# Stacked parts of q and k and rows of routing weights fetched by DMA instead of made by matmuls

## The chip, the cores and the metric

One core of a Trainium2 chip runs the whole kernel. The metric is the device time of one execution in microseconds. The engines run their own instruction streams in order and meet at semaphores: TensorE (PE in the profile), VectorE (DVE), ScalarE (ACT), GpSimd (POOL), and SyncE (SP), which issues DMAs.

## The reference

The input x is 4 batches of 1024 rows of 128 values. Each row is normalised (xn), and two branches work on it; the result is x + s * g.

```python
xn = _layernorm(x, axis=-1)
s = _L0_attn_ref(xn, ...)            # 16 heads of 8 values; q, k, v = xn @ w_qkv + b_qkv
g = _silu(_L0_ffn_ref(xn, ...))      # 16 experts of 64 hidden values, 4 chosen for a row, and a shared one of 128
# attention: heads 0 to 3 causal over all rows; heads 4 to 15 causal over the last 33 rows
# experts: scores = sigmoid(xn @ gate_w.T); the best 2 of 4 groups, in them the best 4 experts,
#          cw = their normalised scores * 2.5, 0 for the rest
y = jnp.einsum('nei,ne,ehi->nh', silu(hg) * hu, cw, Wd)
```

## The kernel before, in words

A batch is handled as two chunks of 512 rows (`CH`); features lie on the 128 partitions, rows on the free axis. The 16 heads are four groups `g` of four; groups 0 to 2 have the windowed heads, group 3 (`GLOBAL`) the causal ones. Each engine walks the same list of steps (`at.steps`) and carries out its own part of each. The list is written out by hand as strings of letters (`FIRST_ORDER`, `BODY_ORDER`, `LAST_ORDER`, L147 to L154), which weave streams: P prepares the next batch, A makes the operands of a group, R is scores and weighted values, X the experts, T the routing, V the values, C the division by the sums, 0 and 1 the output of a chunk. The start is one such list (67 us long), then the middle list runs for batches 0 to 2, each with the preparation of the next batch and its first six expert pairs in it, then the last list.

**Parts of q and k.** Products of q and k must be nearly exact in float16. So q is held as a high part `qkh` and a rest `qkl`, each 128 features by 1024 rows. For a group of four heads an operand has 32 rows for a head: 8 rows for each of three parts (q: high, rest, high; k: high, high, rest), and 8 rows of which one is the constant 1 in k and takes the negative row maximum in q. Before the change TensorE builds these with 0/1 matrices: `qsel` and `ksel` (L614, L615) are two matmuls a chunk, `x_a` with `qkh` and `x_b` with `qkl`, into a PSUM bank that ScalarE copies to `qtmp` and `kall` (L877, L879; for k it adds the constant row). Then `pads` has VectorE spread `qtmp` to the block form `qpad` (L1048), `max` multiplies it with `kall` and takes row maxima (L1144, L1146), `maxdone` has GpSimd lay the maxima on a diagonal (L1211), and `qfull` (L609, L610) adds them to q for the operand `qall`, which `score` uses (L659, L671); `kpads` is VectorE's copy of `kall` to blocks (L1061).

**Experts.** For a pair of experts `up` makes gate and up products, three matmuls each (L513 to L515). ScalarE applies tanh (L809), VectorE forms the product (L1100, then L1109, shown as L916 since a helper records it), GpSimd multiplies it with the routing weights (L1220), and `down` multiplies with `down_w` (L746). The weights `cw` of 16 experts are transposed to `cwT` (`cwT`, L595), with a rest computed by VectorE (L1139), and for a pair one matmul (L730) with `pairsel` spreads two rows of `cwT` over 64 partitions each; ScalarE copies it to `wrow` (L815). Thus an expert step takes three tiles of a ring of three PSUM banks (`EXP`), and the tiles of attention take turns on three others (`ATT`).

**DMAs.** SP loads the inputs, and per batch the next `xin` (L485), `xres` (L488), and two stores of the output (L491).

Of the kernel before, what the change touches and what calls it, by code (L numbers as in the profile page):

```python
# [16 lines left out]
F32 = mybir.dt.float32  # L17
F32R = mybir.dt.float32r
# [39 lines left out]
NWT = 3  # L58
SPLIT_PAIR = 6
XSLOTS = 3  # L60
ROUTE_PARTS = 7
# [3 lines left out]
C16 = {"q_a": HG * P, "q_b": HG * P, "k_a": HG * P, "k_b": HG * P, "negmax": P, "eye": P}  # L65
# [69 lines left out]
def expert_steps(c):  # L135
    out = []
    for t in range(NUP + LAG_DOWN):
# [4 lines left out]
        if t >= LAG_DOWN:  # L142
# [4 lines left out]
FIRST_ORDER = ("PIPPIIIPPPIITPPITPIPTITIPPTPIPPTIPPPPPTIPPIITTVXXVXVXXVXVXVXXXVVXXVXVXX")  # L147
BODY_ORDER = ("AAPAARXAAXAXRRARRAAARAAAAXXRPAAARAAXAXAARRAXRRAAAARRRAXAARAAPXARAAAAAAAXAAARXAAARAXAAAAXXRRRARAR"
              "RAAARAAAAARRARRAAARRRARAXARAAXAXRRRRARAPRAARXRRRRAAAARRRXAXRAXRRRAXRRARARAARPRRPARAXRRXXRTRXRRRR"
              "RTPRTRRRRPRRTXRRRRRRXXXRXRCRPRPRRRXXXRPPRPRRRRRPRRRTPCRRXXRPRRRRRTRRXPRXPRXRPPRRRRRXRRRTXXRRRRRT"  # L150
              "TRPCXPC00XVXXVXXVVVX01XXXX1X1VXVVVVXX")
LAST_ORDER = ("AAAAAAAXAARAARAAAXXRARXRAAAAARRARAAAXAXRRRAXARXAXARAARAAARRARAAAAAAAAAXAARAXAAAXXARAXRRRARRARAAA"
              "RAAAARARAAXRARRXRRRXRRRAAAAAAAARAAAARAAARAXRAXRRAXAAXRRRRAARRXRRRXRRRRRRRRAAXRRRXRXCXRRRRXCRRRRR"
              "RRRRRRXXRRRRRRRXRRRRXRRXRRRRXXRRRRXRRRRR0RXXRRRRRRRXRRRRRRXRRRRRRRXXR0XCC0111")  # L154
# [57 lines left out]
class Section:  # L212
# [5 lines left out]
    def __init__(self, steps):  # L218
# [3 lines left out]
        for s in steps:  # L222
# [8 lines left out]
            if s[0] in ("pv", "down", "norm", "qpads", "z", "z2", "ln", "stats", "pads", "kpads", "maxdone", "ctx", "route", "times",  # L231
                        "mul", "setup", "fill", "ones"):
                continue
            ahead = s[0] in ("qsel", "ksel", "max") and s[1] == 0
            ring = EXP if s[0] in ("up", "weights", "xT", "q", "k", "gate") or ahead else ATT
            parts = [s] if s[0] != "up" else [s + (x,) for x in ("weight", "gate", "up") if x != "weight" or s[2] < EP]
# [48 lines left out]
def build(nc, x, w_qkv, b_qkv, w_out, b_out, gate_w, gate_bias, Wg, Wu, Wd, Ws_g, Ws_u, Ws_d,  # L285
          c32, c16, out):
    with ExitStack() as ctx:
# [16 lines left out]
        def const16(name, g=0):  # L304
            return k16[:, f16at[name][0] + g * P:f16at[name][0] + (g + 1) * P]
# [24 lines left out]
        pairsel = sb("pairsel", [P, EP, P], F32R)  # L330
# [16 lines left out]
        qkl = sb("qkl", [P, 2, S], F16)  # L347
# [954 lines left out]
```

## Time and profile before

| | us |
|---|---|
| median of 3 runs (579.01 to 580.9) | 579.53 |
| the profiled execution | 581.03 |
| its span, first to last instruction | 579.2 |
| TensorE busy | 516.5 |
| VectorE busy | 429.8 |
| ScalarE busy | 332.7 |
| GpSimd busy | 179.6 |

The profile is of one execution. A busy time is the time in which an engine had at least one instruction at work; matmuls overlap, so their durations do not add up to it. The clock that is given for TensorE is the share of full speed that was granted.

### The profile page before, as it was taken

To read this page: it belongs to the slowest core of one execution; us is meant where nothing else is said; L and a number is where in the kernel's file an instruction comes from. 1 tells how busy PE (TensorE), PEld (TensorE's weight loads), DVE (VectorE), ACT (ScalarE), POOL (GpSimd) and SP (SyncE) were. 2 spreads that over 40 slices of the span, in tenths; PEclk is the share of its full clock that TensorE was granted. 3 is DMA by queue.
4 is the path that set the end of the run, shared out by engine and by line. 5 is a ranking of instruction groups with operands and counts; after the bars stand their busy time and mean duration, and the time that the engine had idled before them with its cause. 6 is when DMAs were issued, how large, how long until landed. Compare 5 with 4: busy or idle time off the path is not lost.

```text
span 579.2 us, 10586 instructions
## 1 busy us (share of the span) xinstructions
PE 516.5 (89%) x3930; PEld 301.7 (52%) x3960; DVE 429.8 (74%) x937; ACT 332.7 (57%) x646; POOL 179.6 (31%) x167
## 2 busy tenths in 40 slices
PE   1768999899998999899998999999998999989992
PEld 1636665555445665555445655545454755644440
DVE  6786697786698788886789788786779776877423
ACT  3544556656855457555865367564875457455851
POOL 3413431033524441024423442023342632003311
PEclk9957999998999999998999999998999999999996
DMA  9200000000000300000000300000000110000001
GB/s 233 73 1 0 2 1 1 2 1 2 0 1 2 110 2 2 1 1 1 1 2 1 94 16 3 1 1 1 1 2 0 37 38 1 3 1 0 1 1 36
DMA packets 17933, 9.82 MB, mean 17 GB/s; under 512 B 2502, under 2 KB 17754, under 8 KB 17882
## 3 DMA queue, kind: packets, MB, share of 16 engines
q1 hardware_dynamic: 17552, 8.85, 5.6%
q8 instruction: 31, 0.51, 0.4%
q10 hardware_dynamic: 330, 0.30, 0.3%
q14 instruction: 20, 0.16, 0.1%
HBM read 7.05 MB, written 2.10 MB: 16 GB/s over the span
## 4 chain that ended last, share of the span: by engine, by line
PE 48%; DVE 32%; issue 7%; ACT 6%; DVEq 3%; POOL 2%; DMA 1%; POOLq 0%; ACTq 0%
PE bank L746 6%; DVE kpad L1061 4%; DVE mxp L1146 4%; PE bank L629 4%; DVE mxp L1144 4%; PE bank L513 4%; PE bank L515 4%; PE bank L514 4%; PE bank L690 3%; DVE qpad L1048 3%; PE bank L659 3%; PE bank L706 3%; DVE denT L1085 3%; PE bank L730 2%; DVE hid L1100 2%
## 5 line engine op out<-in xcount | busy, mean ns | idle before, releaser
L889 ACT ACTIVATE stage<-bank 128x512 f32<-128x512 f32 (+3 forms) x240 | 112.7, 521 | 62.8 <-PE bank L663 41.7
L1220 POOL TENSOR_TENSOR hid<-hid,wrow 128x512 f32<-128x512 f32 x64 | 82.2, 1286 | 171.6 <-DVE hid L916 171.6
L1144 DVE TENSOR_REDUCE mxp<-bank 128x1 f32<-128x512 f32 (+4 forms) x192 | 89.8, 517 | 14.0 <-PE bank L632 8.2
L1100 DVE SCALAR_TENSOR_TENSOR hid<-hid,bank 128x512 f32<-128x512 f32 x72 | 48.9, 680 | 54.7 <-ACT hid L809 54.5
L746 PE MATMUL bank<-hid,down_w 128*128 128x512 f32 x144 | 76.0, 609 | 0.0
L1211 POOL TENSOR_TENSOR maxd<-mxp,k 128x512 f16<-128x512 f32 x32 | 36.4, 1137 | 117.9 <-DVE mxp L1146 64.0
L809 ACT ACTIVATE hid<-bank 128x512 f32<-128x512 f32 x72 | 43.3, 601 | 48.2 <-PE bank L515 47.4
L513 PE MATMUL bank<-xh,up_hi 128*128 128x512 f32 x144 | 60.8, 422 | 2.4 <-DVE hid L916 1.8
L514 PE MATMUL bank<-xh,up_lo 128*128 128x512 f32 x144 | 57.8, 401 | 0.0
L515 PE MATMUL bank<-xl,up_hi 128*128 128x512 f32 x144 | 57.4, 399 | 0.0
L659 PE MATMUL bank<-kpad,kall 128*128 128x512 f16 (+3 forms) x192 | 54.8, 329 | 2.1 <-ACT stage L889 1.7
L629 PE MATMUL bank<-kall,qpad 128*128 128x512 f16 (+4 forms) x192 | 50.5, 317 | 5.7 <-DVE mxp L1144 2.6
L916 DVE TENSOR_TENSOR hid<-hid,bank 128x512 f32<-128x512 f32 x72 | 48.9, 679 | 1.3
L659 PEld LDWEIGHTS bank<-kpad,kall 128*128 128x128 f16 x192 | 17.8, 97 | 44.9 <-issue 25.4
L690 PE MATMUL bank<-stage,vg 128*32 128x512 f32 (+3 forms) x384 | 40.0, 497 | 0.0
L815 ACT ACTIVATE wrow<-bank 128x512 f32<-128x512 f32 x64 | 38.1, 596 | 2.8 <-PE bank L730 2.8
L1048 DVE COPY qpad<-qtmp 32x1024 f16<-32x1024 f16 x64 | 29.7, 464 | 12.0 <-ACT qtmp L877 11.3
L730 PE MATMUL bank<-cwT,pairsel 128*128 128x512 f32 x64 | 33.7, 526 | 3.6 <-DVE hid L916 3.1
L882 ACT ACTIVATE qall<-bank 128x512 f16<-128x512 f32 x32 | 18.7, 597 | 31.2 <-PE bank L610 31.2
L513 PEld LDWEIGHTS bank<-xh,up_hi 128*128 128x128 f32 x144 | 28.2, 196 | 11.8 <-DVE hid L916 5.0
L1146 DVE TENSOR_REDUCE mxp<-bank 128x8 f32<-128x512 f32 x48 | 31.9, 686 | 2.8 <-PE bank L641 2.0
L629 PEld LDWEIGHTS bank<-kall,qpad 128*128 128x128 f16 x192 | 17.0, 96 | 31.9 <-DVE mxp L1144 17.4
(162 smaller groups left out, 1002.4 us busy)
## 6 DMA issues: line engine op xcount, KB each, us to landing
xin<-in_L_attn_x_dram SPq DMA_DIRECT2D x4, 512.0 KB, 4.2
xres<-in_L_attn_x_dram SPq DMA_DIRECT2D x4, 512.0 KB, 4.1
out_dram<-xres SPq DMA_DIRECT2D x8, 256.0 KB, 2.3
k<-in_c_dram SPq DMA_DIRECT2D x1, 576.0 KB, 5.8
stage<-in_L_ffn_Wg_dram SPq DMA_DIRECT2D x1, 512.0 KB, 6.0
stage<-in_L_ffn_Wu_dram SPq DMA_DIRECT2D x1, 512.0 KB, 5.9
stage<-in_L_ffn_Wd_dram SPq DMA_DIRECT2D x1, 512.0 KB, 7.4
k<-in_c_dram ACTq DMA_DIRECT2D x1, 216.5 KB, 3.9
```

Of the source, the lines that this page charges most:

```text
L513: pe.matmul(ps[:], w_hi, x_hi, start=True, stop=False)
L514: pe.matmul(ps[:], w_lo, x_hi, start=False, stop=False)
L515: return pe.matmul(ps[:], w_hi, x_lo, start=False, stop=True)
L629: ins = pe.matmul(ps[:, 0:cols], qpad[:, j, :, :], kall[:, g % 2, CH * c:CH * c + cols], start=True, stop=not last, skip_group_check=True)
L659: ins = pe.matmul(ps[:, 0:cols], kall[:, g % 2, P * j:P * (j + 1)], kpad[:, g % 2, q0 // BLK:(q0 + cols) // BLK, h, :], start=True, stop=n ...
L690: ins = pe.matmul(acc[BLK * h:BLK * (h + 1), q0 - CH * c:q0 - CH * c + cols], vg[:, j, h, :], prob[:, (SCORES_BEFORE[g] + m) % NPROB, 0:cols],
L746: pe.matmul(banks[Y][:], down_w[:, t, :], hid[:, i % NHID, :], start=(t == 0), stop=(t == NUP - 1)).then_inc(down_done, 1)
L889: act.activation(prob[:, t % NPROB, 0:cols], ps[:, 0:cols], ACT.Exp).then_inc(freed, 1)
L1100: dve.scalar_tensor_tensor(out=hid[:, i % NHID, :], in0=hid[:, i % NHID, :], scalar=1.0, in1=banks[at.bank(gate)][:], op0=ALU.add, op1=ALU ...
L1144: ins = dve.tensor_reduce(mxp[:, c, j:j + 1], ps[:, 0:cols], AX_X, ALU.max)
L1146: ins = dve.tensor_reduce(mxp[:, 0, LOC * n:LOC * (n + 1)], ps[:].rearrange("p (j q) -> p j q", q=2 * BLK), AX_X, ALU.max)
L1220: pool.tensor_tensor(hid[:, i % NHID, :], hid[:, i % NHID, :], wrow[:, iw % NWT, :], ALU.mult)\
```

## The change

The high parts and rests of q and k of a batch are stored to a DRAM tensor `planes` (for each head four parts of 8 rows), and both operands of a group come back as one transfer each (`strips`), already stacked, since in `planes` the rows of a head stand one behind the other. The fourth part, zeros for q and the constant row for k, is stored once at the start. `qtmp` gets two slots. The routing weights (`cwT`, 16 rows, in float32, halved by ScalarE) are stored to `cw_rows`, and a pair's rows are loaded to `wrow` with each row repeated over 64 partitions; one load covers two pairs, and three such slots are in use. The matmuls L614, L615 and L730, ScalarE's copies of their results (L815, L877, L879) and VectorE's subtraction for `cwT` (L1139) go, as do `pairsel` and the selection matrices. An expert step takes two tiles of its ring. All three orders are written anew. ScalarE and GpSimd get waits before they write what SP still may read. SP now walks the steps too.

```diff
-NWT = 3
+NWS = 3
+LOADS = NCH * EP // 2
+PARTS = 4
...
-C16 = {"q_a": HG * P, "q_b": HG * P, "k_a": HG * P, "k_b": HG * P, "negmax": P, "eye": P}
+C16 = {"negmax": P, "eye": P}
...
-    return ([("qsel", g, c) for c in range(NCH)] + [("ksel", g, c) for c in range(NCH)] + [("pads", g)]
-            + maxes[:half] + [("maxdone", g, 0)] + made + maxes[half:] + [("maxdone", g, 1)])
+    return ([("strips", g), ("pads", g)] + maxes[:half] + [("maxdone", g, 0)] + made + maxes[half:] + [("maxdone", g, 1)])
...
+        def written(b):
+            return 16 * (4 + 6 * b)
...
+            sp.wait_ge(plane_ready, 1)
+            for u in range(2):
+                for w, plane in enumerate((kpad[:, 1].rearrange("p j h q -> p (j h q)")[:, 0:S], maxd[:].rearrange("p j q -> p (j q)"))):
+                    sp.dma_start(planes[2 * u + w, :, PARTS - 1, :, :], plane).then_inc(planes_written, 16)
+
+            def load_weights(n):
+
+                c, t, slot = n // (EP // 2), 2 * (n % (EP // 2)), n % NWS
+                for side in range(2):
+                    row = cw_rows[2 * t + side:2 * t + side + 3:2, chunk(c)]
+                    sp.dma_start(wrow[64 * side:64 * side + 64, 2 * slot:2 * slot + 2, :],
+                                 row.unsqueeze(0).broadcast_to([64, 2, CH])).then_inc(wrow_loaded[slot], 16)
...
+                if at.section is not FIRST:
+                    for c in range(NCH):
+                        sp.wait_ge(stored[c], 16 * b + 16)
+                    sp.dma_start(xres[:], of_batch(x_v, b)).then_inc(xres_loaded, 16)
+                for s in at.steps:
+                    kind = s[0]
+                    if kind in ("q", "k") and s[1] == 1:
+                        w, to = "qk".index(kind), 2 * (at.next % 2) + "qk".index(kind)
+                        sp.wait_ge(lo_ready, at.next * 2 * NCH + (NCH + w + 1))
+                        for part, own in enumerate((qkh, qkl, qkh) if w == 0 else (qkh, qkh, qkl)):
+                            sp.dma_start(planes[to, :, part, :, :], own[:, w, :]).then_inc(planes_written, 16)
+                    elif kind == "strips":
+                        g = s[1]
+                        of, heads = b if g else at.next, slice(4 * HEADS[g], 4 * (HEADS[g] + 1))
+                        sp.wait_ge(planes_written, written(of + 1))
+                        if at.section is not FIRST:
+                            used = ("qfull", (g + 2) % HG, 1) if g != 1 else ("qfull", 0, 0)
+                            sp.wait_ge(emptied[at.bank(used)], at.taken(used))
+                            if g != 1:
+                                sp.wait_ge(kpad_ready, b * GLOBAL + (g - 1 if g else GLOBAL))
+                        for w, to in enumerate((qtmp, kall)):
+                            sp.dma_start(to[:, g % 2, :], planes[2 * (of % 2) + w, heads]
+                                         .rearrange("h a d q -> (h a d) q")).then_inc(strips_loaded[g % 2], 16)
+                    elif kind == "cwT":
+                        c = s[1]
+                        sp.wait_ge(emptied[at.bank(s)], at.taken(s))
+                        sp.dma_start(cw_rows[:, chunk(c)], cwT[:, chunk(c)]).then_inc(cw_rows_stored, 16)
+                        if c == NCH - 1:
+                            sp.wait_ge(cw_rows_stored, 16 * NCH * (at.next + 1))
+                            if at.next:
+                                sp.wait_ge(hid_ready, at.next * NCH * EP)
+                            for n in range(NWS):
+                                load_weights(n)
+                    elif kind == "times" and s[2] < EP and s[2] % 2:
+                        n = (EP * s[1] + s[2]) // 2 + NWS
+                        if n < LOADS:
+                            sp.wait_ge(hid_ready, at.of(s) * NCH * EP + (EP * s[1] + s[2] + 1))
+                            load_weights(n)
...
-                        else:
-                            n = "qk"[w]
-                            pe.matmul(ps[:], const16(n + "_a", g), qkh[:, w, chunk(c)], start=True, stop=False)
-                            ins = pe.matmul(ps[:], const16(n + "_b", g), qkl[:, w, chunk(c)], start=False, stop=True)
...
-                            if x == "weight" and t < EP:
-                                if first:
-                                    all_taken(pe, at, [("cwT", i) for i in range(NCH)])
-                                ps = fill(at, s + (x,))
-                                done(at, s + (x,), pe.matmul(ps[:], pairsel[:, t, :], cwT[:, chunk(c)], start=True, stop=True))
...
-                            act.activation(wrow[:, iw % NWT, :], banks[at.bank(weight)][:], ACT.Copy)\
-                                .then_inc(emptied[at.bank(weight)], 1)
...
+                        elif at.next:
+                            act.wait_ge(planes_written, written(at.next))
...
+                        act.wait_ge(lo_ready, 2 * NCH * (b + (2 if at.section is BODY else 1)))
                         act.activation(sT[:, chunk(s[1])], ps[:], ACT.Identity, bias=bs[:], scale=0.5).then_inc(freed, 1)
...
-                        all_taken(dve, at, [("qsel", g, i) for i in range(NCH)])
+                        dve.wait_ge(strips_loaded[g % 2], 2 * 16 * ((b if g else at.next) * HG // 2 + g // 2 + 1))
...
-                            tt(cwT[32:32 + E, chunk(c)], ps[0:E, :], cwT[0:E, chunk(c)].bitcast(F32), ALU.subtract).then_inc(freed, 1)
...
+                        slot = n % NWS
+                        pool.wait_ge(wrow_loaded[slot], 32 * (at.of(s) * LOADS_OF[slot] + n // NWS + 1))
```

Where the steps stand in the new middle list (the position of 313; before there were 325): `qfull` 0 of the batch 0 and 4, `up` pair 6 at 1, the statistics of the next x at 2, `strips` 1 at 6, `pads` 1 at 9, `up` pair 7 at 10, the first `max` of group 1 at 13, `strips` 2 and `pads` 2 at 30 and 32, `strips` 3 and `pads` 3 at 52 and 53; `q` and `k` of the next batch's second chunk at 194 and 198, `strips` 0 at 202 and `pads` 0 at 234; `cwT` at 274 and 275, `up` pairs 0 to 5 between 281 and 303, the last `times` at 305, and seven steps of V behind it.

## Rows read from the trace of the kernel before

**Rows 1.** The page's part 1: busy time, share of the span, instructions
```profile
PE 516.5 (89%) x3930; PEld 301.7 (52%) x3960; DVE 429.8 (74%) x937; ACT 332.7 (57%) x646; POOL 179.6 (31%) x167
```

**Rows 2.** Windows by batch: stretch, its us, busy us of each engine, clock, DMA
```profile
199.60:332.30 132.70, 124.47 (x975) 72.90 (x982) 104.95 (x231) 80.41 (x157) 43.77 (x37) 0.99 0.05 13
465.00:579.20 114.20, 98.14 (x810) 50.93 (x814) 66.73 (x120) 62.42 (x124) 26.03 (x23) 0.95 0.03 9
0.00:66.90 66.90, 44.63 (x199) 32.20 (x201) 47.80 (x127) 29.14 (x51) 22.17 (x33) 0.85 0.26 67
```

**Rows 3.** Windows, two parts of one middle batch
```profile
200.00:264.00 64.00, 59.52 (x623) 35.59 (x627) 53.47 (x124) 39.02 (x74) 16.46 (x13) 1.00 0.02 6
264.00:332.00 68.00, 64.26 (x353) 37.09 (x352) 50.78 (x107) 41.39 (x83) 27.31 (x24) 0.97 0.06 16
```

**Rows 4.** The page's part 4, chain that ended last, by engine
```profile
PE 48%; DVE 32%; issue 7%; ACT 6%; DVEq 3%; POOL 2%; DMA 1%; POOLq 0%; ACTq 0%
```

**Rows 5.** Groups of TensorE by form: busy us, mean ns | idle before
```profile
L614 PE MATMUL bank<-qkh,k 128*128 128x512 f16 x64 | 25.3, 396 | 2.5 <-DVE up_lo L916 2.2 <-issue 0.2
L615 PE MATMUL bank<-qkl,k 128*128 128x512 f16 x64 | 25.3, 395 | 0.0
L730 PE MATMUL bank<-cwT,pairsel 128*128 128x512 f32 x64 | 33.7, 526 | 3.6 <-DVE hid L916 3.1 <-ACT wrow L815 0.3
```

**Rows 6.** The chain in order of time: start us, us, what
```profile
200.65 0.22 PE bank L614
200.87 0.22 PE bank L615
...
202.10 0.31 PE bank L730
202.41 0.23 PE bank L513
```

**Rows 7.** Groups of ScalarE by form
```profile
L815 ACT ACTIVATE wrow<-bank 128x512 f32<-128x512 f32 x64 | 38.1, 596 | 2.8 <-PE bank L730 2.8
L879 ACT ACTIVATE kall<-bank,k 128x512 f16<-128x512 f32 x32 | 21.1, 692 | 6.9 <-PE bank L615 6.5
L877 ACT ACTIVATE qtmp<-bank 128x512 f16<-128x512 f32 x32 | 17.5, 601 | 4.7 <-PE bank L615 4.7
```

**Rows 8.** Groups of VectorE by form
```profile
L916 DVE TENSOR_TENSOR cwT<-bank,cwT 16x512 fp32r<-16x512 f32 x8 | 5.2, 676 | 2.2 <-ACT cwT L856 2.2
L1048 DVE COPY qpad<-qtmp 32x1024 f16<-32x1024 f16 x64 | 29.7, 464 | 12.0 <-ACT qtmp L877 11.3
```

**Rows 9.** The page's part 6: DMA issues, KB each, us to landing
```profile
xin<-in_L_attn_x_dram SPq DMA_DIRECT2D x4, 512.0 KB, 4.2
out_dram<-xres SPq DMA_DIRECT2D x8, 256.0 KB, 2.3
```

**Rows 10.** Timelines of one batch turn: start us, us, engine, line
```profile
176.45 1.05 ACT L856 ACTIVATE cwT<-bank 16x512 fp32r<-16x512 f32 x2
...
185.00 2.56 POOL L1220 TENSOR_TENSOR hid<-hid,wrow 128x512 f32<-128x512 f32 x2
...
195.65 0.51 SPq L485 DMA_DIRECT2D xin<-in_L_attn_x_dram  x1
...
199.63 0.38 PE L609 MATMUL bank<-qtmp,k 128*128 128x512 f16 x1
...
204.37 1.71 DVE L1048 COPY qpad<-qtmp 32x1024 f16<-32x1024 f16 x4
```

**Rows 11.** Windows: the start's DMA, and where the granted clock fell
```profile
6.00:12.00 6.00, 0.68 (x3) 0.60 (x3) 5.18 (x25) 1.65 (x4) 1.65 (x1) 1.00 1.14 313
27.00:30.00 3.00, 1.13 (x7) 0.60 (x6) 2.61 (x8) 2.03 (x4) 1.45 (x2) 0.92 0.00 0
30.00:33.00 3.00, 1.82 (x4) 0.13 (x2) 2.61 (x15) 0.99 (x2) 0.00 (x0) 0.50 0.00 0
268.00:270.00 2.00, 2.00 (x4) 0.69 (x4) 1.14 (x4) 1.02 (x2) 0.63 (x1) 0.62 0.00 0
```

More of the change, by code:

```diff
@@ L231, in __init__ @@
             if s[0] in ("pv", "down", "norm", "qpads", "z", "z2", "ln", "stats", "pads", "kpads", "maxdone", "ctx", "route", "times",
-                        "mul", "setup", "fill", "ones"):
+                        "mul", "strips", "setup", "fill", "ones"):
                 continue
-            ahead = s[0] in ("qsel", "ksel", "max") and s[1] == 0
+            ahead = s[0] == "max" and s[1] == 0
             ring = EXP if s[0] in ("up", "weights", "xT", "q", "k", "gate") or ahead else ATT
-            parts = [s] if s[0] != "up" else [s + (x,) for x in ("weight", "gate", "up") if x != "weight" or s[2] < EP]
+            parts = [s] if s[0] != "up" else [s + (x,) for x in ("gate", "up")]
             for part in parts:
@@ L402, in build @@
         sums_ready = sem("sums_ready")
-        cw_hi_ready = sem("cw_hi_ready")
+        cw_rows_stored = sem("cw_rows_stored")
+        wrow_loaded = [sem(f"wrow{slot}_loaded") for slot in range(NWS)]
         small_loaded = sem("small_loaded")
@@ L419, in build @@
         kpad_ready = sem("kpad_ready")
+        plane_ready = sem("plane_ready")
+        planes_written = sem("planes_written")
+        strips_loaded = [sem(f"strips{i}_loaded") for i in range(2)]
         qg_ready = sem("qg_ready")
@@ L494, in _ @@
-            for b in range(B - 1):
-                batch(At(BODY, b))
-            batch(At(LAST, B - 1))
+                if at.section is not FIRST:
[36 more added lines that the diff above has]
+                            load_weights(n)
+                    elif kind == "outT":
+                        c = s[1]
+                        sp.wait_ge(emptied[at.bank(s)], at.taken(s))
+                        sp.dma_start(of_batch(out_v, b)[:, TPC * c:TPC * (c + 1), :], xres[:, TPC * c:TPC * (c + 1), :])\
+                            .then_inc(stored[c], 16)
@@ L497, in _ @@
+            sections(sp, walk)
             for c in range(NCH):
@@ L855, in walk @@
                         else:
-                            act.activation(cwT[0:E, chunk(s[1])], banks[at.bank(s)][0:E, :], ACT.Copy).then_inc(cw_hi_ready, 1)
+                            if at.next:
+                                act.wait_ge(cw_rows_stored, 16 * NCH * at.next)
+                            act.activation(cwT[:, chunk(s[1])], banks[at.bank(s)][0:E, :], ACT.Copy, scale=0.5)\
+                                .then_inc(emptied[at.bank(s)], 1)
                         continue
-                    if kind not in ("xT", "q", "k", "gate", "qsel", "ksel", "qfull", "score", "proj"):
+                    if kind not in ("xT", "q", "k", "gate", "qfull", "score", "proj"):
                         continue
@@ L1057, in walk @@
                             continue
-                        all_taken(dve, at, [("ksel", g, i) for i in range(NCH)])
                         for h in range(4):
@@ L1112, in walk @@
                         continue
-                    elif kind in ("weights", "small", "vbias", "vn", "v", "cwT", "max", "outT"):
+                    elif kind in ("weights", "small", "vbias", "vn", "v", "max", "outT"):
                         ps, freed = banks[at.bank(s)], emptied[at.bank(s)]
@@ L1200, in walk @@
                         pool.wait_ge(emptied[at.bank(s)], at.taken(s))
+                        if at.next and c == 0:
+                            pool.wait_ge(planes_written, written(at.next))
                         pool.tensor_tensor(qkl[:, w, chunk(c)], qkf[:, w, :], qkh[:, w, chunk(c)], ALU.subtract)\
```

106 lines of the change are left out of this document (38 added, 68 removed).

## The prediction

> **What bounds the kernel now.** I read the page's busy line first. TensorE is busy for 516.5 of 579.2 us, VectorE for 429.8, ScalarE for 332.7, GpSimd for 179.6 [rows 1]. An average can hide stages, so I cut the span at the starts of the batches. They repeat every 132.7 us: in each of the three middle batches TensorE is busy for about 124.5 us, VectorE for 105.0, ScalarE for 80.4. The last batch takes 114.2 us (TensorE 98.1, VectorE 66.7), and the start 66.9 us, of which TensorE is busy for only 44.6 [rows 2]. So the batches are bound by TensorE, at 94%. Then I cut a batch in two: in its first 64 us (window attention and the search for row maxima) VectorE is busy for 53.5 us, that is 84%, beside TensorE's 59.5; in the other 68 us the two have 50.8 and 64.3 [rows 3]. TensorE leads everywhere, VectorE is close behind it in the first half. The chain that ended last agrees: 48% of it on TensorE, 32% on VectorE, 6% on ScalarE, 1% on DMA [rows 4].
>
> **What goes from TensorE.** In each batch the selection of q and k takes 4 tiles for each of 4 groups of heads, at two matmuls a tile: 32 matmuls (L614, L615; 128 in the run), and 16 matmuls that spread the routing weights (L730; 64) [rows 5]. The mean durations there (396 and 526 ns) overlap, since matmuls are pipelined; what one costs is the distance to the next on the chain: 0.22 us for a selection, 0.31 for a spread where the next is another kind, against 0.23 for an ordinary matmul of its size [rows 6]. So a middle batch loses 32 x 0.216 = 6.9 us and 16 x 0.23 to 0.31 = 3.7 to 5.0 us; I take 4.3, together 11.2 us. The last batch loses the selections of three groups, 24 x 0.216 = 5.2, and 10 spreads, 2.7: 7.9 us. The weight loads go along with them; they lie beside matmuls.
>
> **What goes from the others.** ScalarE loses 64 copies of spread weights at 596 ns and 32 + 32 evictions of selections at 692 and 601 ns [rows 7], about 19 us of a batch's 80. It is not the bound, so I give nothing for the busy time itself; it does make tanh and exp start sooner. VectorE loses only the 8 subtractions for cwT, 676 ns each: 1.4 us a batch [rows 8]. Its copies to qpad and kpad stay. After the change it has 103.6 us of work a batch. The three banks for experts now take two tiles a step instead of three, which loosens TensorE's waits for banks; from above the 8 us in which it is idle in a batch [rows 2] bound that, I take 0.
>
> **What is added.** All of it is DMA on SP's queue: per batch 6 stores of 256 KB (three parts of q, three of k), 8 loads of 256 KB (two for each group), 2 small stores of routing rows and 16 loads of 256 KB that repeat a row over 64 partitions. Rows show 512 KB landing in 4.2 us and a 256 KB store in 2.3 [rows 9], and one issue taking 0.5 us of SP [rows 10]; at 36 issues, 18 us a batch, SP is far from full. The 30 transfers of 256 KB are 7.9 MB a batch. Each piece costs only where an engine reaches its wait before it lands:
> - Routing weights. cwT is out of ScalarE in the row at 176.45; GpSimd's first multiplication starts at 185.00 [rows 10]. Store and load need 2.3 + about 3 us after ScalarE's end at 177.5, so they land near 183 to 184: hidden. The other rows are prefetched six experts ahead. Below: 0; above: 3 us where the batch turns; I take 0.
> - Group 0 of the next batch (k's second tile to its pads): ScalarE and GpSimd about 2.6 us, stores 3.6, loads 4, so 10 us. Between the two steps the new order has 11 score tiles, 3 groups of weighted values, 2 experts and 2 down projections, about 10.7 us of TensorE. Just hidden: 0 to 3 us, I take 0.
> - Groups 2 and 3 can be fetched as soon as the operand tile of two groups earlier is made; nothing slow stands before them on SP: 0.
> - Group 1 is the weak place. Its loads wait for ScalarE's eviction of the first operand tile of the batch, about 1.1 us after the batch starts, and stand on SP behind the last weight loads, xin and xres. Those 1.5 MB and its own 0.5 MB need 6.7 us at the 313 GB/s that the start shows [rows 11], and the first bytes move about when the batch starts. Group 1 then lands some 7 us into the batch, VectorE copies for 1.7 us [rows 10], and max(1,0) runs at 8.7, where TensorE has some 6.3 us of work before it. Queued behind VectorE's pads(1) are the gating of expert pair 7 and all maxima of the group, and GpSimd and TensorE wait for those. I charge 2 us a batch, between 0 and 5.
> - New waits of ScalarE and GpSimd before writing qkf, qkl and sT ask for stores and subtractions of long before: 0.
>
> The whole order is also written anew. With less TensorE work VectorE's share of the first half rises to about 90%, and in-order queues lose something by that: 1.2 us a batch, 0 to 5. A middle batch thus gives 11.2 - 2 - 1.2 = 8 us, the last 7.9 - 1.9 = 6.
>
> In the start TensorE waits for others, so 8 selections and 6 spreads (about 5 us at the clock there) are worth little as such. The routing parts now all come before the weights, which brings cwT forward, but group 0 has to go out and back through DRAM. I take 2 us of gain, between 6 lost and 5 won.
>
> **The sum.** 3 x 8 + 6 + 2 = 32 us. 579.2 - 32 = 547.2, and 1.8 us lie around the span of the profiled execution (581.03), so 549.0. That execution is 1.5 us above the median of the runs: 547.5 us. A measurement tells about 0.3% (1.7 us) from no change.
>
> **Rivals.**
> - VectorE takes over in the first half. For: 84% busy there with work that stays [rows 3], and chains such as copies to kpad, maxima, GpSimd, operand tile. Against: it idles for 10 of the 64 us, and the removed ScalarE steps shorten the same chains. Then the 5.2 us of selections there and some 1.6 us of spreads win nothing: 3 x 4.4 + 1.7 + 0 = 15 us, so about 564.5.
> - The queue at the turn of a batch: slower. From cwT to group 1's landing 12 weight loads, an out of 512 KB, xin, xres and two strips are moved, 5.2 MB, in the 27 us from 176.45 to the copy to qpad at 204.37 [rows 10]. At the rate of the start, 313 GB/s with many transfers in flight [rows 11], that is 17 us and fits. If each 256 KB cost the 2.3 us of a store by itself [rows 9], for instance because 64 copies of one DRAM row are read slowly, it would be 46 us, 19 too late at each of four turns against 10 of gain. It decides from about 12 us of lateness, a rate under 135 GB/s. Half of that worst case: 590 to 600, I name 595. The rate in the rows speaks against it.
> - TensorE's clock. In the start TensorE was busy for 1.13 of 3 us, and the granted clock went to 0.50, the lower level of 1.2 GHz; at 268 us too it was 0.62, in a stretch in which TensorE was busy throughout [rows 11]. A wait for group 1 at every turn could do the same where now the clock is 1.0. At half the clock, 5 us of matmuls a turn cost 5 more; four turns, with waits twice as long as I charge, give 547.5 + 20 + 8 = 575; with half of it, 562. Against: TensorE has work to within 2 us of the wait.
>
> The Trainium skill (TensorE: Matmul & The Clock Gate, Why this matters for your kernels) advises against idle gaps of TensorE between bursts because the clock drops back; the rows just given agree that it drops after little work. By that rule the third rival holds as soon as the wait grows. The Trainium skill (DMA: Bandwidth & Descriptors, Measured) has 138 GB/s for a transfer of 64 KB and 341 for 1 MB, which would put the 5.2 MB between 38 and 15 us; no row here shows a 256 KB load by itself, and by the lower figure the second rival would hold.
>
> **How the numbers follow.** My forecast, 547.5 with its own range 538 to 557, has a chance of 0.60. More than that (banks and ScalarE's sooner starts paying too, 532 to 538): 0.05. VectorE taking over: 0.17. The clock: 0.05. The queue: 0.13. Low end 532, since all TensorE terms in full, 3 x 11.2 + 7.9 + 5, are 46.5 us. High end 574: it holds the VectorE case and most of the clock's and leaves out the queue's. Faster by over 0.3%: 0.60 + 0.05 + 0.17 + 0.03, less 0.02 for mishaps, is 0.83; no change 0.04, slower 0.13.
>
> **What would show it.** L614, L615, L730 gone and a batch period near 124.7 us; TensorE's busy time down by about 45 us, VectorE's by 5. The wait of the copy to qpad for DMA, about 2 to 4 us at each batch start and little elsewhere; GpSimd's multiplications not waiting for DMA. If VectorE leads, its share in the first 64 us passes 93% and the period stays above 127. If the queue decides, wrow's loads take over 5 us to land and pads(1) waits over 8 us. If it is the clock, slices at 0.5 appear after the start of batches. I am wrong outright if the period does not fall below 130.

## The result and the profile after

| | before | after |
|---|---|---|
| median, us (4 runs each) | 580.21 (579.01 to 582.41) | 560.76 (558.08 to 561.4) |
| ratio | | 0.9649 [0.9615, 0.9684] |
| profiled execution, its span | 581.03, 579.2 | 558.08, 556.1 |

The change makes the kernel 19.5 us faster. The forecast was 32 us, to 547.5: the direction and the whole range (532 to 574) hold. The size of the gain is 60% of the forecast, and the time lies outside the forecast's own range (538 to 557), nearer to the 564.5 of the rival in which VectorE takes over. The profiled execution of after lies 2.7 us below its median, so its trace shows 23 us of gain.

The page after: busy time of each engine, the chain by engine, and the DMA issues (KB each, us to landing); they answer to [rows 1, 4, 9].

```profile
PE 472.3 (85%) x3768; PEld 277.6 (50%) x3768; DVE 439.5 (79%) x930; ACT 267.7 (48%) x517; POOL 178.2 (32%) x166
...
DVE 43%; PE 33%; issue 6%; POOL 5%; ACT 4%; DVEq 4%; DMA 4%; SPq 1%; POOLq 0%; ACTq 0%
...
wrow<-cw_rows SPq DMA_DIRECT2D x64, 256.0 KB, 4.5
planes<-qkh SPq DMA_DIRECT2D x16, 256.0 KB, 3.4
qtmp<-planes SPq DMA_DIRECT2D x16, 256.0 KB, 3.1
kall<-planes SPq DMA_DIRECT2D x16, 256.0 KB, 4.1
xin<-in_L_attn_x_dram SPq DMA_DIRECT2D x4, 512.0 KB, 5.9
...
out_dram<-xres SPq DMA_DIRECT2D x8, 256.0 KB, 4.3
```

TensorE lost 44.2 us of busy time, where 45 were forecast for its removed matmuls. ScalarE lost 65; its removed copies last 76.7 us when they are added up one by one [rows 7]. VectorE lost its 8 subtractions, 5.2 us [rows 8], yet its busy time rose by 9.7. It also leads the chain now, 43% against TensorE's 33%; before it was 32 to 48 [rows 4].

The windows of after: one row for each batch, then two middle batches in halves (stretch, its us, busy us of PE, PEld, DVE, ACT, POOL, clock, DMA share, GB/s). They answer to [rows 2, 3].

```profile
0.00:62.90 62.90, 37.07 (x186) 28.16 (x187) 48.42 (x127) 22.23 (x40) 22.49 (x33) 0.95 0.53 148
62.90:190.40 127.50, 114.97 (x934) 67.10 (x934) 108.47 (x229) 64.44 (x125) 43.65 (x37) 0.99 0.26 75
190.40:320.50 130.10, 113.89 (x935) 66.24 (x936) 108.22 (x228) 64.45 (x125) 43.61 (x37) 1.00 0.26 74
320.50:449.80 129.30, 114.99 (x934) 67.84 (x934) 108.33 (x228) 64.46 (x125) 43.68 (x37) 0.99 0.26 75
449.80:556.10 106.30, 91.36 (x780) 48.31 (x780) 66.10 (x119) 52.14 (x102) 24.73 (x22) 0.96 0.12 36
...
190.40:257.40 67.00, 56.89 (x628) 34.95 (x629) 57.50 (x128) 31.08 (x58) 17.68 (x15) 1.00 0.18 57
257.40:320.50 63.10, 57.00 (x309) 31.29 (x309) 50.72 (x100) 33.38 (x67) 25.93 (x23) 1.00 0.34 92
```

Where the 23 us come from: the start gives 4.2 (the middle list begins at 62.9 instead of 67.1), the three middle batches 132.6 us against 127.5, 130.1 and 129.3, together 11.0, and the last batch 7.9. The forecast had 2, 24 and 6. So the whole shortfall lies in the middle batches: 3.7 us each instead of 8. Inside one of them most of it lies in the first half. Set by the same matmul, the last operand tile of group 3, the half took 67.8 us before and takes 66.0, 67.0 and 67.8 us in the three batches after, though about 6 us of TensorE's busy time has gone from it in the batch shown (62.9 before, 56.9 after). The second half took 64.9 and takes 61.5, 63.1 and 61.6: it gives back some 2.8 us for the 4.5 that went from TensorE there. In the first half neither engine is full, TensorE 85% and VectorE 86%. That points at a chain between the two; the experiments test it.

The turn of a batch in after, start us, us, engine, line (in brackets the idle time before, and what ended it). The batch starts at 320.49.

```profile
316.70 1.23 SPq L501 DMA_DIRECT2D wrow<-cw_rows  x2
...
317.98 0.59 SPq L508 DMA_DIRECT2D xin<-in_L_attn_x_dram  x1
...
324.26 1.65 DVE L1047 BATCH_NORM_STATS2 top<-xin 128x6 f32<-128x128 f32 x8 [1.13 <-DMA xin<-in_L_attn_x_dram]
...
326.95 1.78 POOL L1217 TENSOR_TENSOR y<-ve,half 128x8 f32<-128x8 f32 x1 [10.27 <-DVE ve L948]
...
327.41 2.69 DVE L1077 COPY qpad<-qtmp 32x1024 f16<-32x1024 f16 x4
328.55 1.26 POOL L1249 TENSOR_TENSOR hid<-hid,wrow 128x512 f32<-128x512 f32 x1
...
330.15 0.39 PE L680 MATMUL bank<-kbf 128*128 128x512 bf16 x1 [2.27 <-DVE qpad L1077]
```

`xin` is issued 2.5 us ahead of the batch, where before it was 4.0 [rows 10]: on SP it stands behind row loads, which ask for the multiplication that empties their slot. It lands 5.9 us after its issue (the median) instead of 4.2. VectorE's statistics wait for it, and group 1's copies to `qpad` stand behind the statistics. They take 2.69 us for four instead of 1.71 [rows 10], beside a multiplication of GpSimd, and TensorE waits. Group 1's first operand tile is issued 15.3 us into this batch, before it was 10.2.

### The profile page after: what moved, and what is told of

It is laid out like the page before. It is cut to its first block, busy times and chain, and to the rows that moved or that the text cites. A ratio compares the mean times of both kernels' runs of the same rounds, so it can differ in the third digit from the quotient of the medians.

```text
span 556.1 us, 10169 instructions
## 1 busy us (share of the span) xinstructions
PE 472.3 (85%) x3768; PEld 277.6 (50%) x3768; DVE 439.5 (79%) x930; ACT 267.7 (48%) x517; POOL 178.2 (32%) x166
## 4 chain that ended last, share of the span: by engine, by line
DVE 43%; PE 33%; issue 6%; POOL 5%; ACT 4%; DVEq 4%; DMA 4%; SPq 1%; POOLq 0%; ACTq 0%
DVE mxp L1171 6%; DVE qpad L1077 5%; DVE kpad L1089 4%; PE bank L783 4%; DVE mxp L1173 4%; DVE denT L1116 3%; DMA xin<-in_L_attn_x_dram 3%; PE bank L674 3%; DVE hid L1131 3%; DVE hid L945 3%; PE bank L735 3%; PE bank L704 3%; PE bank L570 3%; PE bank L751 2%; PE bank L572 2%
## 5 line engine op out<-in xcount | busy, mean ns | idle before, releaser
L1239 POOL TENSOR_TENSOR maxd<-mxp,k 128x512 f16<-128x512 f32 x32 | 36.1, 1129 | 128.2 <-DVE mxp L1173 83.9
L570 PE MATMUL bank<-xh,up_hi 128*128 128x512 f32 x144 | 67.9, 472 | 3.8 <-DVE mxp L1173 1.8
L571 PE MATMUL bank<-xh,up_lo 128*128 128x512 f32 x144 | 56.6, 393 | 0.0
L1077 DVE COPY qpad<-qtmp 32x1024 f16<-32x1024 f16 x64 | 34.1, 532 | 4.7 <-DMA kall<-planes 4.0
L910 ACT ACTIVATE qall<-bank 128x512 f16<-128x512 f32 x32 | 19.1, 598 | 37.7 <-PE bank L661 37.5
L680 PE MATMUL bank<-kbf 128*128 128x512 bf16 x48 | 18.8, 393 | 17.3 <-DVE qpad L1077 17.3
L863 ACT ACTIVATE ctxT<-bank 32x512 f32<-32x512 f32 x24 | 14.1, 587 | 37.3 <-PE bank L751 37.2
```

The costliest lines, as they stand in the source:

```text
L570: pe.matmul(ps[:], w_hi, x_hi, start=True, stop=False)
L571: pe.matmul(ps[:], w_lo, x_hi, start=False, stop=False)
L1077: ins = dve.tensor_copy(qpad[r, :, h, :], qtmp[r, g % 2, :].rearrange("p (j q) -> p j q", q=BLK))
```

## The experiments

Each was timed beside the kernel before; its median on these chips was 579.8 to 580.4 us. A kernel differs from after only by its diff (two from before, as said). "Operand tile of group 1" is the time of the first matmul of that tile from the start of a middle batch: 10.2 us in before, 13.0 to 15.3 in after.

### a_nostrips: the transfers of q's and k's parts gone

```diff
-                        for part, own in enumerate((qkh, qkl, qkh) if w == 0 else (qkh, qkh, qkl)):
-                            sp.dma_start(planes[to, :, part, :, :], own[:, w, :]).then_inc(planes_written, 16)
...
-                        for w, to in enumerate((qtmp, kall)):
-                            sp.dma_start(to[:, g % 2, :], planes[2 * (of % 2) + w, heads]
+                    pool.memset(qtmp[:], 0.125)
+                    pool.memset(kall[:], 0.125)
```

> The kernel after, with no transfer of q and k parts at all: their stores, the loads of the stacked operands and every wait for them are left out, and the operands are constants. Turn theory (group 1 lands late at each batch turn, 5 us at its first operand tile): the batch period falls from 129 to about 125 us and the time to about 547. VectorE theory (the first half of a batch is bound by VectorE, the lateness is covered by that): the period stays above 127.5 and the time at 555 to 559. The start would gain 0 to 3 us in both.

560.90 us, ratio 0.9656 [0.9628, 0.9684]: the same as after, and so neither the 547 of the turn theory nor quite the 555 to 559 of the other. The operand tile of group 1 comes at 15.2 to 15.6 us. Fetching q and k through DRAM costs nothing, not even at the turn, where I had charged it 2 us a batch.

### b_norows: the loads of routing rows gone

```diff
-                            for n in range(NWS):
-                                load_weights(n)
...
-                            sp.wait_ge(hid_ready, at.of(s) * NCH * EP + (EP * s[1] + s[2] + 1))
-                            load_weights(n)
```

> The kernel after, with no loads of routing rows: GpSimd multiplies by a constant tile. It leaves out the 64 transfers that repeat DRAM rows. If these clog the queue at the batch turn (4.5 us each to land), xin and group 1 come 3 us sooner: 550. If queue time is not what counts: 557 to 561.

552.36 us, ratio 0.9503 [0.9473, 0.9533], 8.4 us below after. Period 126.7 us, operand tile of group 1 at 12.6, and `xin` has landed when it is wanted. It is the row loads that stand in the way, as bytes or as waits on SP.

### c3_both and c1_queue: xin ahead of the row loads

In c1_queue `xin` is issued where q of the next batch's first chunk is made and `xres` in the middle of the batch, both off the turn. In c3_both group 1 is fetched together with group 0 as well, into a third slot of `kall` (to make room, the two chunks of `cwT` lie one above the other on the partitions).

```diff
-                if at.section is BODY:
-                    sp.wait_ge(xl_ready, NCH * b + NCH)
-                    sp.dma_start(xin[:], of_batch(x_v, b + 1)).then_inc(x_loaded, 16)
...
+                    if s == ("q", 0) and at.next < B - 1:
+                        sp.wait_ge(xl_ready, NCH * at.next + NCH)
+                        sp.dma_start(xin[:], of_batch(x_v, at.next + 1)).then_inc(x_loaded, 16)
+                    if s == ("up", 1, 0) and at.section is not FIRST:
...
+                        sp.dma_start(xres[:], of_batch(x_v, b)).then_inc(xres_loaded, 16)
```

> The kernel after with the turn of the batch cleared: group 1's operands are fetched together with group 0's, into a slot of their own of kall, xin is loaded when the x before it has been used, and xres in the middle of a batch. Nothing is left out. Turn theory: VectorE's first copies to qpad run some 5 us sooner in a batch, period about 125, time about 548. VectorE theory: period 127 to 128.5, time 554 to 558.

> The kernel after with xin loaded as soon as the x before it is used, and xres in the middle of a batch; group 1 is fetched as in after. If xin's lateness is all of the turn's loss, this equals the variant that also fetches group 1 ahead: 552 to 556, first operand tile of group 1 at 12.6 us of a batch. If group 1's own lateness is a part: 557 to 559.

c3_both: 554.08 us, 0.9548 [0.9519, 0.9577]. c1_queue: 553.86 us, 0.9548 [0.9521, 0.9575]. They are equal, so group 1's own fetch is worth nothing and `xin` is worth the whole 6.9 us. In both the operand tile of group 1 comes at 12.6 us in every batch. One batch of c1_queue in halves and the first half of the next, same columns as above:

```profile
192.14:257.74 65.60, 58.42 (x629) 35.99 (x630) 57.40 (x128) 31.09 (x58) 17.73 (x15) 0.97 0.18 55
257.74:320.65 62.91, 56.81 (x309) 31.25 (x309) 50.73 (x100) 33.39 (x67) 25.88 (x23) 1.00 0.35 97
...
320.65:386.23 65.58, 56.90 (x628) 34.95 (x629) 57.38 (x128) 31.09 (x58) 17.73 (x15) 1.00 0.17 50
```

The half is 65.6 us long, 2.2 less than before; the wait for DMA is gone, and still the half gives back only a third of TensorE's 6 us. In the first of these batches the granted clock was at its lower level for 3.4 us (0.97 over the half), and TensorE was busy for 58.4 us; in the first half of the two others it was busy for 56.9, and all three are 65.6 us long. So here 1.5 us more of TensorE's time cost nothing. c1_queue computes all of the reference, and is the fastest kernel here that does.

### k_stats: the statistics moved behind group 1's first maxima

On top of c3_both, one step of the middle list is moved later:

```diff
-BODY_ORDER = ("AXPXARARXAXRRAARAAARRRRAAAAXRPAXAXAARXRRAAARAAARXRXAAAAAAAAPRAAAXRAAAXAARXAAAXXRRARARXAAARARRAAR"
+BODY_ORDER = ("AXXARARXAXRRAARAAPARRRRAAAAXRPAXAXAARXRRAAARAAARXRXAAAAAAAAPRAAAXRAAAXAARXAAAXXRRARARXAAARARRAAR"
```

> The variant with both (group 1 ahead, xin early), with the statistics of the next x moved from the second step of a batch to behind group 1's first maxima. VectorE's 3.2 us of statistics stood ahead of the copies to qpad. If VectorE's place in line is what bounds the first 15 us: the first operand tile of group 1 at about 9.5 us, 2 to 3 us less a batch, 544 to 549. If its total work bounds the whole first part, the time is only moved: 552 to 555.

561.89 us, 0.9693 [0.9667, 0.972]: 7.8 us worse than c3_both. Group 1's first operand tile comes sooner (11.5 us), the second later (17.0), and the period is about 130 us. The 3 us of statistics ahead of group 1 are not lost time; moved behind it they hold up its second half, with a GpSimd step of 1.6 us (L1217 of after, from the statistics) ahead of its maxima. Both expectations, a gain and no change, fell.

### d_oldorder: the changed kernel in the order of before

```diff
-FIRST_ORDER = ("IPIIPPPPIPPPPTPTTTTITTIVPIIIVTIIPIPPTPIPPPPXXXXXXXXXXXXXXXIIVVVVVVVV")
-BODY_ORDER = ("AXPXARARXAXRRAARAAARRRRAAAAXRPAXAXAARXRRAAARAAARXRXAAAAAAAAPRAAAXRAAAXAARXAAAXXRRARARXAAARARRAAR"
+FIRST_ORDER = ("PIPPIIIPPPIIITPPITPIPTITIIPPTPIPPTIPPPPPTIPPIITTVXXVXVXXVXVXVXXXVVXXVXVXX")
+BODY_ORDER = ("AAPAARXAAXAXRRARRAAARAAAAXXRPAAARAAXAXAARRAXRRAAAARRRAXAARAAPXARAAAAAAAXAAARXAAARAXAAAAXXRRRARAR"
...
```

> The kernel after with the three orders of the kernel before (the first step of each group's selection becomes its fetch, the other three fall away). If the new order is what puts VectorE and GpSimd in each other's way (VectorE's busy time rose by 10 us although its work shrank), the old order gives 550 to 556 with VectorE busy near 425. If the new order is needed to hide the transfers, the old one is slower than after: 563 to 575, with waits for DMA ahead of the copies to qpad.

626.12 us, 1.0779 [1.074, 1.0819]: slower than before by 46 us, than after by 65. Its batches take 144 to 147 us. The turn of one of them, columns as in the turn above; the batch starts at 208.91:

```profile
210.79 1.55 SPq L501 DMA_DIRECT2D wrow<-cw_rows  x2
212.40 0.58 SPq L508 DMA_DIRECT2D xin<-in_L_attn_x_dram  x1
...
213.93 2.87 SPq L530 DMA_DIRECT2D qtmp<-planes  x1
...
219.15 1.65 DVE L1047 BATCH_NORM_STATS2 top<-xin 128x6 f32<-128x128 f32 x8 [9.79 <-DMA xin<-in_L_attn_x_dram]
222.26 1.70 DVE L1077 COPY qpad<-qtmp 32x1024 f16<-32x1024 f16 x4
224.02 0.10 PEld L680 LDWEIGHTS bank<-kbf 128*128 128x128 bf16 x1 [9.60 <-DVE qpad L1077]
224.02 0.61 PE L680 MATMUL bank<-kbf 128*128 128x512 bf16 x1 [9.48 <-DVE qpad L1077]
```

Here the multiplication that empties the last row slot comes after the next batch has begun, and `xin` is issued 3.5 us into the next one instead of 2.5 us ahead of it. VectorE waits 9.8 us for it, TensorE 9.5 us, and the granted clock from 222 to 228 us is 0.54 (0.61 us for that matmul instead of 0.39). SP's waits in this stretch (us in total, times, longest) name what held `xin`:

```profile
SPq L501 <- POOL hid L1249: 7.4, 2, 5.8
```

This is the prediction's rival of the queue, as a wait on SP and not as a low rate: the row loads land in 4.4 us there too. The order of the steps alone decides whether it shows. In the whole run the copies to `qpad` wait 31.1 us for DMA, against 4.0 in after, and the mean granted clock is 0.91 against 0.98. The forecast for an unfit order (563 to 575) was far too low. One sign of the other expectation came true all the same: VectorE is busy for 427.5 us, 12 less than in after with the same instructions, so it is the new order that sets VectorE and GpSimd more often side by side.

### e_undo_sel: the selections by TensorE again, in the new order

```diff
-    return ([("strips", g), ("pads", g)] + maxes[:half] + [("maxdone", g, 0)] + made + maxes[half:] + [("maxdone", g, 1)])
+    return ([("sel", g), ("pads", g)] + maxes[:half] + [("maxdone", g, 0)] + made + maxes[half:] + [("maxdone", g, 1)])
...
+                        pe.matmul(ps[:], const16(n + "_a", g), qkh[:, w, chunk(c)], start=True, stop=False)
+                        done(at, s, pe.matmul(ps[:], const16(n + "_b", g), qkl[:, w, chunk(c)], start=False, stop=True))
```

> The kernel after with the selections made by TensorE again (128 matmuls of 0.22 us, 64 evictions by ScalarE, at the place where the fetches stood) and the routing rows still by DMA. If TensorE's time counts everywhere, 8.6 us come back in each middle batch's first and second part: 560.8 + 28 = 585 to 590. VectorE theory (in the first 66 us of a batch TensorE's time is free): only group 0's 1.7 us a batch and the last batch count, 563 to 572, with the third operand tile of a batch at 13 to 16 us as in after.

This kernel also has `qtmp` in one slot again. 591.79 us, 1.0187 [1.0149, 1.0226]: 31 us above after. The VectorE theory, in which TensorE's time in the first half is free (563 to 572), fell; the time lies even above the 585 to 590 of the other. TensorE's busy time rises by 34.3 us, the period to 137 us; the copies to `qpad` wait 25.7 us in all for ScalarE's `qtmp`. The period grows by about what TensorE's busy time grows by (34.3 us over four batches are 8.6; the period rises by 7 to 9.6). But the selections bring back ScalarE's copies ahead of VectorE's too, and in before the copies to `qpad` waited 11.3 us for them, not 25.7 [rows 8]. How much of the 31 us is TensorE's time, how much the longer chain through ScalarE, and how much this order not fitting the old work stays open.

### f_undo_rows: the spreads by TensorE again, in the new order

```diff
+                            if x == "weight" and t < EP:
+                                if first:
+                                    all_taken(pe, at, [("cwT", i) for i in range(NCH)])
+                                ps = fill(at, s + (x,))
+                                done(at, s + (x,), pe.matmul(ps[:], pairsel[:, t, :], cwT[:, chunk(c)], start=True, stop=True))
...
+                            act.activation(wrow[:, iw % NWT, :], banks[at.bank(weight)][:], ACT.Copy)\
```

> The kernel after with the routing weights spread by TensorE again and q and k parts by DMA. TensorE gets 64 x 0.23 to 0.31 us back, 15 to 20 us in all, ScalarE 38 us; but the row loads are gone from the queue at the batch turn, which are worth up to 8 us. TensorE theory: 570 to 577. If the loads cost about what the matmuls did: 560 to 566.

579.06 us, 0.9972 [0.9949, 0.9994]: 18.3 us above after, 25.2 above c1_queue. The second is the fair comparison, since with the row loads `xin`'s wait went too (the operand tile of group 1 at 12.8 us). The period is 132.3 to 133.7 us against c1_queue's 127.2 to 128.5, that is 5.0 us a batch for 16 spreads; forecast 4.3, upper bound 5.0. Of these 5.0 us the second half has 3.9. The rest of the 25.2 us lies in the start (7.1) and the last batch (3.0). Both ranges set for this run (570 to 577, 560 to 566) were too low; the 25.2 us are also more than the 20.6 us by which TensorE's busy time rose against c1_queue.

### g_relief_after and h_relief_before: half of VectorE's copies to the pads left out

g is from after, h the same edit in before, at both loops of copies:

```diff
-                        for h in range(4):
+                        for h in range(2):
```

> The kernel after with VectorE making only two of the four copies of each qpad and kpad block form (left out: heads 2 and 3 of every group); 56 of 112 copies go, about 32 us of VectorE, 8 us a batch, of which 6.5 in the first 66 us. VectorE theory: 540 or less, at least 5 us a batch. If TensorE or the transfers bound the first part: 553 to 559.

> The kernel before with the same half of the copies to qpad and kpad left out. It is the yardstick for the one above: VectorE theory says that before the change VectorE's time counted less, so a gain of 1 to 3 us a batch, 568 to 576. If the gain is as large as in the changed kernel (20 us), VectorE bound the first part before the change too.

g: 538.36 us, 0.9281 [0.925, 0.9311], 22.4 us below after, for 26.6 us less of VectorE's busy time. h: 567.17 us, 0.9751 [0.9714, 0.9788], 12.7 below before, for 25.4 less. The forecasts, 540 or less and 568 to 576, were met and missed by 0.8 us. So a microsecond of these copies is worth 0.84 us now and was worth 0.50 before: before, "bound by TensorE" was already half untrue, and the change moved the bound towards VectorE. These copies stand on the way to TensorE's maxima, so other work of VectorE may be worth less.

### i_pool_after and j_pool_before: GpSimd's multiplications made short

i is from after, j the same edit in before (L1220):

```diff
-                        pool.tensor_tensor(hid[:, i % NHID, :], hid[:, i % NHID, :], wrow[:, 2 * slot + t % 2, :], ALU.mult)\
+                        pool.tensor_tensor(hid[:, i % NHID, 0:64], hid[:, i % NHID, 0:64], wrow[:, 2 * slot + t % 2, 0:64], ALU.mult)\
```

> The kernel after with GpSimd's multiplication by routing weights made on 64 of 512 columns (the rest is left out); it takes 1.29 us 64 times otherwise. In after many copies to qpad last 1.4 us instead of 0.41, beside such a multiplication. If GpSimd's work holds VectorE up: those copies have a mean near 465 ns instead of 532, VectorE's busy time falls by 8 to 15 us, and the time by 5 to 12, to 549 to 556. If not: VectorE's durations stay and the time is 557 to 561.

> The kernel before with the same multiplication on 64 columns. There the copies to qpad already have their short duration (464 ns mean). If the change put VectorE in GpSimd's way more than before, the gain here is smaller than in the changed kernel: 576 to 580, VectorE's busy time down by less than 6 us.

i: 541.67 us, 0.9344 [0.9316, 0.9371], 19.1 us below after. j: 572.11 us, 0.9855 [0.9825, 0.9885], 8.0 below before. Both gain more than was expected (549 to 556 and 576 to 580). Not one instruction of VectorE was changed, and its busy time falls by 15.3 us in i (to 424.2) and by 7.9 in j. Why, the groups by form show (busy us, mean ns of one, idle before). First the kernel before:

```profile
L916 DVE TENSOR_TENSOR cmp<-cmp,k 128x128 f32<-128x128 f32 x4 | 1.5, 363 | 0.5 <-issue 0.3
L916 DVE TENSOR_TENSOR msk<-sc,gt 128x128 f32<-128x128 f32 x4 | 1.2, 293 | 0.3
...
L916 DVE TENSOR_TENSOR eq<-msk,top 128x128 f32<-128x128 f32 x4 | 1.1, 279 | 0.0
```

The same groups, the copies to `qpad` and what waits for them, in after:

```profile
L1077 DVE COPY qpad<-qtmp 32x1024 f16<-32x1024 f16 x64 | 34.1, 532 | 4.7 <-DMA kall<-planes 4.0
L945 DVE TENSOR_TENSOR eq<-msk,top 128x128 f32<-128x128 f32 x4 | 4.3, 1086 | 0.0
L945 DVE TENSOR_TENSOR msk<-sc,gt 128x128 f32<-128x128 f32 x4 | 3.9, 978 | 0.3
L945 DVE TENSOR_TENSOR cmp<-cmp,k 128x128 f32<-128x128 f32 x4 | 3.9, 977 | 0.4
...
L680 PE MATMUL bank<-kbf 128*128 128x512 bf16 x48 | 18.8, 393 | 17.3 <-DVE qpad L1077 17.3
L1047 DVE BATCH_NORM_STATS2 top<-xin 128x6 f32<-128x128 f32 x32 | 6.5, 275 | 2.7 <-DMA xin<-in_L_attn_x_dram 2.7
```

And in i_pool_after:

```profile
L1077 DVE COPY qpad<-qtmp 32x1024 f16<-32x1024 f16 x64 | 28.3, 443 | 2.2 <-DMA kall<-planes 1.6
L945 DVE TENSOR_TENSOR cmp<-cmp,k 128x128 f32<-128x128 f32 x4 | 4.8, 1207 | 0.4
L945 DVE TENSOR_TENSOR eq<-msk,top 128x128 f32<-128x128 f32 x4 | 1.5, 374 | 0.0
L945 DVE TENSOR_TENSOR msk<-sc,gt 128x128 f32<-128x128 f32 x4 | 1.2, 292 | 0.3
```

`eq` and `msk<-sc` fall back to near their old length, `cmp<-cmp,k` stays long. The timeline says what stood beside each. After, one batch (start us, us):

```profile
267.04 1.17 POOL L1229 TENSOR_TENSOR qkl<-sT,qkh 128x512 f16<-128x512 f32 x1 [3.42 <-ACT qkh L905]
...
273.09 1.32 POOL L1249 TENSOR_TENSOR hid<-hid,wrow 128x512 f32<-128x512 f32 x1
...
283.35 1.37 POOL L1249 TENSOR_TENSOR hid<-hid,wrow 128x512 f32<-128x512 f32 x1 [3.18 <-DVE hid L945]
...
267.45 0.90 DVE L945 TENSOR_TENSOR cmp<-cmp,k 128x128 f32<-128x128 f32 x1
...
273.21 1.35 DVE L945 TENSOR_TENSOR eq<-msk,top 128x128 f32<-128x128 f32 x1
283.67 1.21 DVE L945 TENSOR_TENSOR msk<-sc,gt 128x128 f32<-128x128 f32 x1
```

And i_pool_after, the same places:

```profile
262.04 1.17 POOL L1229 TENSOR_TENSOR qkl<-sT,qkh 128x512 f16<-128x512 f32 x1 [4.56 <-ACT qkh L905]
262.14 1.21 DVE L945 TENSOR_TENSOR cmp<-cmp,k 128x128 f32<-128x128 f32 x1
...
268.10 0.37 POOL L1249 TENSOR_TENSOR hid<-hid,wrow 128x64 f32<-128x64 f32 x1
268.21 0.41 DVE L945 TENSOR_TENSOR eq<-msk,top 128x128 f32<-128x128 f32 x1
```

Each of the three long VectorE instructions begins while an instruction of GpSimd runs, and ends 0.14 to 0.16 us after that one's end: 267.04 + 1.17 = 268.21 against 268.35, 273.09 + 1.32 = 274.41 against 274.56, 283.35 + 1.37 = 284.72 against 284.88. A 0.3 us instruction is held until GpSimd is done. In i the multiplication beside `eq` is short, and so is `eq`; the one beside `cmp<-cmp,k` is the rest of q and k, which i did not touch, and `cmp` lasts 1.21 us. The Trainium skill (SBUF — State Buffer, SBUF: two separate sides) calls the port pair that VectorE and GpSimd share "an exclusive lock, not a bandwidth split", held for the whole instruction; the trace agrees.

The whole of it can be added up from the traces: for every VectorE instruction that runs beside one of GpSimd, the time above the shortest of its form (where it is more than 0.08 us). That is 26.8 us in before and 41.5 in after, 29.2 in d_oldorder, 25.8 in i and 18.6 in j. The difference of 14.7 is nearly the whole rise of VectorE's busy time (9.7, and the 5.2 of the subtractions). By what stood beside it, the multiplications hold VectorE for 9.2 us in before and 18.1 in after, the rests of q and k for 5.5 and 10.7, and the maxima on the diagonal (L1239, L1211 before) for 12.1 in both. Not every instruction is held: the two that form the expert product read a PSUM bank, 28 of their 144 begin beside a GpSimd instruction in after, and all of them last 0.62 to 0.69 us.

The 19 us of i are not all this: i shortens GpSimd's own link between VectorE and the down projections too (GpSimd has 1% of the chain there, 5% in after), and the two were not taken apart.

## Why the prediction was right in direction and too large in size

**Right.** L614, L615 and L730 are gone and TensorE's busy time fell by 44.2 us (45 forecast). The spreads measured 5.0 us a batch, at the upper bound of the term (4.3 taken), with ScalarE's copies in it. The loads of routing rows are hidden as such: GpSimd waits 3.2 us for them over the whole run. Groups 0, 2 and 3 fetch their parts at no cost (a_nostrips). Start and last batch, 4.2 and 7.9 us, came out above the 2 and 6 forecast. That the time lies in the range at all is owed to its high end, which was set to hold the VectorE rival. Of the signs that were named, the period (127.5, 130.1 and 129.3 us) is far from 124.7 and in one batch at the 130 from which the prediction calls itself wrong, and VectorE's busy time rose by 9.7 us instead of falling by 5.

**The step that failed: VectorE's "1.2 us a batch".** It is the larger part of the miss. A middle batch was to give 11.2 us from TensorE; in c1_queue, where nothing waits for a late transfer at the turn, the three together take 383.3 us instead of 397.9, 4.9 each. So 6.3 us a batch are withheld where I took 1.2 (TensorE's own busy time fell by 10.5 a batch there, which accounts for 0.7 of them). Two things were wrong in it. I took VectorE's work as 103.6 us a batch; it measures 108.3, since more of its two-input instructions and copies meet one of GpSimd's and are held. And I priced its nearness as a loss from in-order queues, not by what a microsecond of VectorE is worth: 0.50 before, 0.84 after (g, h). How the 6 us divide between the two isn't shown. Nor is it shown that VectorE withholds all of them. Put back, TensorE's work costs in full (e: 31.0 us for 34.3 of busy time; f against c1_queue: 25.2 for 20.6), and since the old work was never run whole in the new order, a part of the 6 us can be a price of that order by itself.

**The step with the wrong cause: "I charge 2 us" for group 1's fetch.** Its size was about right (6.9 us over three middle batches), its transfer wrong. I had put `xin` ahead of group 1 on SP and asked only when group 1's parts would land, not when `xin` itself is issued: on SP it is behind row loads that wait for GpSimd's multiplications, and on VectorE its statistics stand before group 1's copies. a_nostrips (nothing) and c1_queue (6.9 us) show it, and c3_both equals c1_queue. The lateness varies (13.0, 14.0 and 15.3 us in after's profiled execution, which was 2.7 us below its median; 15.2 to 15.6 in every middle batch of a_nostrips).

**Rivals.** "VectorE takes over" (564.5, chance 0.17) described the mechanism better than the forecast did: the first half gains 0.2 to 1.9 us of the 6.8 that it was to give. Its test was only half met. The period stays above 127, but VectorE's share of the first half is 86%, not over 93: two engines that hand work to each other bind a stretch in which neither is full. The queue's rival did not come: row loads land in 4.5 us, under its 5, and the copies to `qpad` wait 4.0 us for DMA in the whole run, not 8 at each turn. (The prediction says that by its lower figure for the rate this rival would hold. That figure lies just above the limit of 135 GB/s that the prediction works out itself, so by its own sum the rival would not quite hold.) d_oldorder shows that it was nearer than its 0.13 suggests, and by another mechanism: it decides by the order of steps. I gave that order, a large part of the diff, no gain or loss but the 1.2 us; it is worth 65 us between d_oldorder and after. The clock's rival shows a little. In three of after's four batches the granted clock is at its lower level for 3.4 us, 11 to 16 us behind the start, each time after a wait of TensorE for group 1 (2.1 to 2.3 us); the second batch has such waits of 2.4 and 2.1 us and no fall. Behind the one of the turn above:

```profile
328.50:336.50 8.00, 6.28 (x108) 5.22 (x108) 7.05 (x11) 1.08 (x3) 2.47 (x3) 0.79 0.00 1
```

The granted clock was 0.79 in these 8 us. Over the batch it was 0.99, as in before, where each middle batch has such a stretch of 3.4 us too, but at its middle; so it cost little.

## What to carry to other kernels

Before pricing what leaves the leading engine, measure what a microsecond of the second one is worth (leave out part of its work and time it): with TensorE at 93% and VectorE at 84% of the first half, a microsecond of VectorE's copies was worth half a microsecond here. When a queue gets waits that it did not have, follow the old transfers behind them, not only the new ones; moving `xin` ahead of the row loads gives 6.9 of the 553.86 us kernel's 26 us. A busy time that rises although work was taken away is a sign of instructions held by another engine: compare the mean of each form with its shortest. And an order that was fitted to one mix of work is not neutral for another: the same instructions ran in 560.8 and in 626.1 us.

## What the runs showed of the hardware

- A VectorE instruction with two inputs (128x128 f32, 0.28 us alone) beside a GpSimd one lasts to 0.14 to 0.16 us past that one's end, up to 1.38 us; a copy of 32x1024 f16 lasts to 0.28 us past it and goes from 0.41 to 1.42 us. It counts as busy time in the profile, so a busy VectorE is not one at work (26.8 us of 429.8 in before, 41.5 of 439.5 in after). Instructions of 128x512 with one input in PSUM kept their 0.62 to 0.69 us beside GpSimd.
- A 256 KB load of two routing rows repeated over 64 partitions lands in 4.5 us, a fetch of stacked parts in 3.1 to 4.1, a store of a part in 3.4 (medians of after). `xin`'s 512 KB went from 4.2 to 5.9 us among them, and to 4.3 when issued apart from them (c1_queue).
- SP needs 0.3 to 0.7 us for nearly every issue in after, but 2.87 us for one of d_oldorder's behind row loads, `xin` and `xres`.
